# Graph layer kernel: five more edge groups through an eighth count table, and the stages' spread over the steps redrawn

## What is computed

```python
xn = _layernorm(x, axis=-1)
x = x + gcn(xn, src, dst) + linear_attention(xn)      # both residual branches read xn
x = x + mixture_of_experts(_layernorm(x, axis=-1))    # 8 experts, best 2 of each row
# gcn: h = x @ W; norm = dinv[src]*dinv[dst]
#      out = segment_sum(h[src] * norm[:, None], dst) + bias, normalised over everything, PReLU
```

## Time and profile before

| | us |
|---|---|
| median of three executions | 1534.99 |
| lowest and highest | 1532.45, 1539.14 |
| the profiled execution | 1534.88 |
| its span, first to last instruction | 1532.9 |
| first gather to last gather of the step phase | 172.2 to 820.5 |

### The profile page before, as it was taken

The page is one execution under the profiler, slowest core; times in us unless marked ns, Lnnn a source line. Parts: engine busy times, 40 slices in busy tenths (PEclk is TensorE's granted clock), DMA queues, the critical chain, the costliest instruction groups (busy, mean ns, idle before and its releaser), DMA issues. The chain is left out here.

```text
span 1532.9 us, 30179 instructions
## 1 busy us (share of the span) xinstructions
PE 1266.2 (83%) x8310; PEld 1107.0 (72%) x8311; DVE 960.1 (63%) x2700; ACT 450.8 (29%) x1322; POOL 764.0 (50%) x822
## 2 busy tenths in 40 slices
PE   1797678888888999998987978767999999999910
PEld 1685477887787889887775856523999999999900
DVE  3998777777688888778854977863222223222347
ACT  1565600122123333333221023463322332233200
POOL 2001577777777777777774023201555555555400
PEclk9999898999999999999998989955999999999965
DMA  6002533333466667778895000252666666666658
GB/s 204 15 0 69 168 106 105 104 105 106 126 177 174 199 196 215 211 219 261 279 283 166 1 1 1 108 181 94 211 210 209 216 209 210 212 215 207 192 198 314
DMA packets 142678, 248.24 MB, mean 162 GB/s; under 512 B 22826, under 2 KB 99108, under 8 KB 142324
## 3 DMA queue, kind: packets, MB, share of 16 engines
q1 hardware_dynamic: 99256, 146.13, 29.8%
q0 software_dynamic: 34320, 93.76, 21.0%
q10 hardware_dynamic: 9004, 7.21, 1.4%
HBM read 213.65 MB, written 33.36 MB: 161 GB/s over the span
## 5 line engine op out<-in xcount | busy, mean ns | idle before, releaser
L716 POOL DMA_INDIRECT RG<-table,srci x504 | 496.0, 984 | 157.7 <-issue 154.4
L733 PE MATMUL ps<-S_t,RG 128*128 128x96 f32 x2016 | 283.7, 278 | 51.7 <-DMA RG<-table,srci 47.8
L733 PEld LDWEIGHTS ps<-S_t,RG 128*128 128x128 f32 x2016 | 270.3, 195 | 74.8 <-DMA RG<-table,srci 60.8
L1881 DVE TENSOR_TENSOR R<-ps,R 128x256 f32<-128x256 f32 x105 | 44.6, 425 | 278.4 <-PE ps L1833 278.4
L1823 PE MATMUL ps<-R,RG 128*128 128x128 f32 x1680 | 207.2, 277 | 0.0
L987 DVE TENSOR_TENSOR R<-R,ps 128x392 f32 x280 | 157.0, 561 | 79.3 <-PE ps L743 59.7
L755 PE MATMUL ps<-zrow,R 128*128 128x256 f32 x686 | 193.3, 386 | 12.8 <-DMA zrow<-table 7.9
L1856 ACT ACTIVATE R<-ps,RG 128x128 f32<-128x128 f32 x420 | 119.7, 368 | 279.0 <-PE ps L1823 279.0
L1833 PE MATMUL ps<-R 128*128 x840 | 198.6, 380 | 0.0
L1823 PEld LDWEIGHTS ps<-R,RG 128*128 128x128 f32 x1680 | 198.4, 194 | 0.0
L1907 POOL DMA_INDIRECT results<-R,S_t x105 | 103.7, 988 | 164.0 <-DVE R L1881 160.8
(11 more groups left out here) (352 smaller groups left out, 1883.3 us busy)
## 6 DMA issues: line engine op xcount, KB each, us to landing
RG<-in_w SPq DMA_DIRECT2D x106, 514.0 KB
zrow<-table SPq DMA_DIRECT2D x336, 128.0 KB
R<-results SPq DMA_DIRECT2D x48, 256.0 KB, 12.2
RG<-table,srci POOLq DMA_INDIRECT x504, 3.4
table<-RG SPq DMA_DIRECT2D x12, 512.0 KB, 2.9
table<-R SPq DMA_DIRECT2D x12, 512.0 KB, 3.3
out<-R ACTq DMA_DIRECT2D x48, 128.0 KB, 5.4
R<-in_x SPq DMA_DIRECT2D x6, 896.0 KB
```

What stands on the lines that cost most here:

```text
L716: nc.gpsimd.indirect_dma_start(out=grows[:, s, :], out_offset=None, in_=table, in_offset=bass.IndirectOffsetOnAxis(ap=srci[:, ND + q, c:c ...
L733: last = nc.tensor.matmul(window(q % 2)[:, h, :], grows[:, s, h * P:(h + 1) * P], S_t[:, q % 2, c, :], start=c == 0, stop=c == GC - 1)
```

## The change

An eighth block, groups 70 to 74, goes through a count table, so `ND` is 75, `MD` (chunks counted) 300 where it was 280, and `GQ` 121. The steps of all stages are redrawn to fit.

```diff
-DBLK = ((0, 27), (27, 38), (38, 46), (46, 53), (53, 59), (59, 65), (65, 70))
+DBLK = ((0, 27), (27, 38), (38, 46), (46, 53), (53, 59), (59, 65), (65, 70), (70, 75))
...
-        A0, A1 = 0, 16
-        C0, C1 = 18, 45
-        B0, B1 = 48, 100
-        D0, D1 = 102, GQ
-        BUILT = (0, 45, 63, 76, 88, 98, 108, 116)
-        USED = (45, 63, 76, 88, 98, 108, 116, GQ - 1)
+        A0, A1 = 0, 14
+        C0, C1 = 16, 41
+        B0, B1 = 45, 98
+        D0, D1 = 100, GQ
+        BUILT = (0, 41, 55, 67, 78, 88, 98, 106, 113)
+        USED = (41, 55, 67, 78, 88, 98, 106, 113, GQ - 1)
```

## The result

The changed kernel takes 1542.4 us (median of 20 executions) where the kernel before takes 1534.9 in the same rounds: a ratio of 1.0048, with a 95% interval from 1.0036 to 1.0059. It is slower by 7.5 us, half a per cent, and the interval excludes no change. The forecast was 1519 us. One of the twenty executions took 1752.3 us at a mean granted clock of 0.743 and is left out of the ratio.

A forecast was written before the change was run, and what follows sets the result against it. POOL's gathers (1.25 us each) set the pace, with PE close behind in the middle and DMA at the end. 1534.9 - (139.95 - 120.5) + 2.5 + 0.8 = 1518.8, so 1519 us; own range 1513 to 1527, eight in ten 1509 to 1531.

The forecast's parts named there:

- The share of 0.93 and the 290 to 300 GB/s: Sign of being right: over the last 100 us, DMA share at 0.93 or more and 290 to 300 GB/s.
- a loop of rings: Sign of being wrong: the last 21 steps take above 130 us, where 120.5 us was forecast.
- the third rival: Gain eaten by late steps of 6.7 and 6.1 us (1537), or by one-hots holding up gathers (1532); chance 0.24, one-hots 0.05.
- 14 x 5.85: Steps 106 to 119: 1.74 MB a step at 298 GB/s needs 5.85 us each; bounds 5.5 and 6.7.
- 6 x 5.6: Steps 100 to 105: 5.6 us each, from 5.50 us of transfers and POOL's 5.5 us with long gathers.
- four separate limits: Late steps: DMA transfers 5.85 us, table ring of six 5.4, loop through SP's queue 5.5, DVE's work 5.0.
- 298 GB/s: DMA rate assumed for the last steps, between the 286 seen at share 0.91 and 314 at full share.
- The rival that I had called slower: SP's in-order queue becomes a loop of waits over steps 106 to 119, from 7.5 us a step: 1542 and above; chance 0.07.
- DVE in steps 45 to 54 "at nothing": DVE has 4.8 us of work a step, covered by POOL's 5.1, costed at nothing; perhaps 3 us if slack spoils.
- 2.5 for PE: PE, above POOL's 5.1 us in twenty steps instead of ten, enters the last part 2.5 us later; bounds 0 and 6.
- The argument on slack: POOL may run four steps ahead; it loses up to 4 us of slack by step 98, so stalls little or not.
- The bandwidth rule: The skill's 358 GB/s a core would mean no DMA bound; rejected for rows showing 286 at 0.91, near 314 full.

The follow-up runs named there:

- before_even_2: The kernel before (seven blocks, 126 steps) with x tiles on ACT's queue and products spread evenly: 1531.1 us, ratio 0.9985 to the kernel before.
- redraw_early_2: The changed kernel with x tiles on ACT's queue and steps redrawn so the blocks begin at step 38: 1514.2 us, ratio 0.9875 to the kernel before.
- x_on_act: The changed kernel with the x tiles issued from ACT's queue instead of SP's: 1532.0 us, ratio 1.0001 to the kernel before.
- mid_built: The changed kernel with one number moved, `BUILT[1]` 39 instead of 41: 1535.4 us, ratio 1.0012 to the kernel before.
- redraw_act: The changed kernel with products spread more evenly over the steps and x tiles on ACT's queue: 1522.9 us, ratio 0.993 to the kernel before.
- x_first: The changed kernel with a step's x tiles ahead of its table tiles in SP's list: 1588.1 us, ratio 1.036 to the kernel before.

## Why the prediction was wrong

**Right.** POOL is the pacemaker before, a step costs 5.1 us, five steps fewer are worth some 25 us on POOL. before_even_2 (2 us of gain without the block) and redraw_early_2 (26.5 us between first and last gather) show both. Of the signs that I named, PE's wait for `zrow` above 13.4 us came true (22.6 on the weight loads), POOL waited little before step 100 (12.8 us for PE, never above 1.1), and step 100 began at 684.5 us for 682. The share of 0.93 and the 290 to 300 GB/s failed (0.81 to 0.91, 250 to 273). And a sign of being wrong came true: the last 21 steps of POOL took some 132 us (from 684.5 to 1.25 behind the start at 815.1), above the 130 that I had set for a loop of rings. Also right: the other work moved onto PE, DMA and DVE; the form of the third rival in which new one-hots hold up gathers did not come (gathers have a median of 946 ns still, and their mean fell from 984 to 968 ns). The excess of the long gathers, which I had left as it was, fell by some 9 us, from 504 x 38 to 484 x 22 ns; it gave nothing, since POOL waited for PE.

**The step that failed: "14 x 5.85", and "6 x 5.6" ahead of it.** I had taken the largest of four separate limits (DMA 5.85, ring 5.4, loop 5.5, DVE 5.0) for steps 106 to 119. Measured, the twenty steps from group 100 on take 6.65 us each, 132.9 us; my sum had meant some 113, since it put the last add 16 us ahead of 832.1 and group 100 at 702.6. The first six of them, from 100 to 106, take 6.6 us each as well as the other fourteen. That is 19.5 us of the some 24 by which the forecast was low. The experiments divide them: 9.1 us are the queue (132.9 to 123.8 with x on ACT), and 9.2 more come off with half the bytes of the table tiles (123.8 to 114.6). 114.6 is about what I had written down, but I had written it for whole tiles: my 298 GB/s were not reached at this density with x on either queue (258 from 700 to 800 us in the changed kernel, 282 in x_on_act).

The limits were all there and named, and the error was to take the largest of them. Queue and bytes each cost time beside the other. My reading, which no run shows by itself, is that a landing delayed by full DMA engines stands inside the loop through SP, ACT, DVE and PE, so that the waits follow each other. The rival that I had called slower was this loop, and I gave it 0.07 because I judged the loop to fit into 5.5 us. The steps took 6.66. I had written that the x tiles go out only when PE has begun their step; at the boundary of step 113 SP spent 8.4 us on the seven tiles ahead of them. That the time landed on this rival's 1542 us is luck: it had asked for 7.5 us a step over fourteen steps; the rest came from the six steps ahead of them and from the middle. In size the third rival's sum, 6.7 and 6.1 us a step and 1537 us, was nearer.

In the prediction's own terms, which followed POOL: step 100 began 0.6 us earlier than the sum had it, the last part took some 132 us for 120.5, and from the last gather to the last add passed 25.5 us where 11.6 had passed before. These 14 us I had put at nothing: POOL may run four steps ahead, so more than half of what PE lost shows only behind the last gather.

**The second: DVE in steps 45 to 54 "at nothing".** By the prices of the earlier trace rows it had 4.8 us of work in 5.1. Measured, steps 49 to 52 take 5.18 us with DVE busy 0.92, so the price was right, and the add of group 52 is only 1.7 us behind. But the boundary of step 55 finds DVE late, and the add of group 56 is 8.9 us behind. The loss of 5 us above what I had put for PE (group 100 at 707.7, forecast 702.6) is this one: mid_built takes 6.4 us off there. Group 100 is 8.4 us later than before; I had 2.5 for PE and 0.8 for the boundary, and 6.8 at the upper bound. What I had not priced is that a late DVE meets a boundary, where PE stops for it, and the clock that falls at the stop. How much each of the two costs was not taken apart.

**The argument on slack** was half right: POOL did run ahead through the loss of the middle (the gathers of step 78 start at 569.2 us in both kernels), but this only postpones. What PE lost at step 55, in a phase where it has 4.7 to 5.3 us of work in 5.1, it had not won back by group 100 (8.9 us behind at group 56, 8.4 at group 100).

**The bandwidth rule** stays open in one direction: redraw_act moved 306 GB/s at a share of 0.98 from 770 to 800 us, near the 314 that I had worked out for a full share:

```profile
770.00:800.00 30.00, 26.99 (x156) 21.53 (x156) 15.68 (x40) 8.40 (x14) 21.34 (x22) 1.00 0.98 306
```

By the figure of the Trainium skill (HBM Reference, Specifications: about 358 GB/s a core) there would have been no bound at 306 GB/s; the share of 0.98 speaks for the row.

## What to carry to other kernels

Where several resources are close to the pace, as here, the price of a step can be above the largest of them: look for the loop that passes through all, and price it with the waits at their loaded length. An in-order DMA queue that serves two rings with different releasers can block one through the other in either order, as it did here in x_first and in the changed kernel; in the kernel before it cost nothing. Consider a queue for each before making a step denser, and spread the tiles so that no step takes as many as a ring holds (the long steps stood behind such steps; that they come of them was not tried). Taking work off the pacemaker pays only as far as the work given to the others is spread evenly: here the same eighth block was 7 us slower or 18 us faster, by the tuples and the queue.

## What the runs showed of the hardware

A short stop of PE can cost more than its length: at the 1.73 us wait of the boundary, PE busy 4.66 of 7 us, the granted clock fell to 0.50; it was 0.50 from 461 to 466 us, and matmuls took twice as long. In mid_built, with a wait of 1.05 us and PE busy 5.95 of the same 7 us, it stayed at 1.00. The changed kernel has it again at 785 to 790 us, with no wait longer than 1.05 us but several, PE busy 6.97 of the 10 us before. And one chip of the same kind ran the kernel before in 1673 us instead of 1533: matmuls that follow one another took as long (eight of the aggregation in 1.03 us, as here), but waits between engines were longer, some of which the profile calls "remote". The mean granted clock was also lower, 0.904 to 0.918 in the four kernels profiled there, where the same kernels had 0.931 to 0.934 elsewhere. What makes the waits so was not tried.
